# Group-normalised, quantised grouped convolution on one core: one transfer over all 128 partitions, and PSUM sets in rotation

## The chip, the cores and the metric

The kernel runs on one core of a Trainium2 chip. The metric is the time of one execution on the device in microseconds (us). The core has five engines that run side by side (TensorE "PE", VectorE "DVE", ScalarE "ACT", GpSimd "POOL", SyncE "SP"), and 16 DMA engines that move data between HBM and the on-chip memory SBUF. Transfers are issued here from two queues, SP's and ACT's. PSUM is the memory into which PE writes.

## The reference

The input `x` has shape (32, 512, 28, 28) in float32. It is group-normalised over 32 groups of 16 channels, and the result `v` goes through a grouped 1x1 convolution with 4 groups of 128 channels:

```python
v = group_norm(x, 32 groups, eps=1e-5)
xg = v.reshape(B, G, Cg, H, W)[:, [1, 2, 3, 0]]        # output group g reads input group g + 1
xa = round(clip((xg - lA) / (uA - lA), 0, 1) * 15) / 15
wq = (round(clip((w - lW) / (uW - lW), 0, 1) * 15) / 15 - 0.5) * 2
y  = einsum('bgihw,goi->bgohw', xa, wq)
out = x + relu(y * inv + (beta - mean * inv)) + v
```

51.4 MB are read and 51.4 MB are written. Everything passes through SBUF once.

## The kernel before

**Layout.** An image (one of the 32) has 512 channels of 784 values. Its four groups lie in `images[P, RING, G, HW]` with two channels of one group in one partition: a pair of neighbouring channels is 6272 contiguous bytes in HBM and in a partition. The 128 partitions are halved (LOW is 0 to 63, HIGH is 64 to 127), and the four slots of a partition are two pairs `y` of two channels `t`. LOW holds group 0 in pair 0 and group 3 in pair 1; HIGH holds group 1 in pair 0 and group 2 in pair 1 (`GROUPS`, L51). The distance in HBM from pair 0 to pair 1 differs between the halves, so each transfer covers one half: 64 partitions with two rows of 6272 bytes each (L234 loads, L214 stores). The first two images and the last one are moved in finer pieces (L222, L246).

**Ring.** 12 images (`RING`) fit in SBUF. `load(n)` (L229) waits from image 12 on until image n - 12 has been stored. Loads are issued by SP. Stores of images 0 to 29 are issued by ACT, and those of images 30 and 31 by SP after all the loads.

**Work for an image.** Mean and variance are taken on DVE (`bn_stats`, L517) and ACT (L274, L282), and are averaged over the channels of a norm group by small matmuls on PE for two images at a time (`average_means` L638, `average_deviations` L651). POOL turns them into coefficients. ACT and POOL quantise to integers (L310, L481), DVE caps them into `codes` (L532), PE multiplies (`multiply`, L679), and POOL (on the last three images ACT too) applies the affine part of the identity in place (L470, L318). At last DVE adds the rectified product onto the image (`finish`, L539), and the image is stored. The statistics run `AHEAD` = 5 images ahead of `finish`. On ACT the store of image n is issued after the statistics of image n + 5 or n + 6, which wait for that image's load.

**PE's order.** `multiply` is done twice for an image (t = 0 and 1), each 3 parts x 2 x 2 x 4 = 48 matmuls of 64 x 64 weights onto 392 columns, four of them on the four quarters of the array, and each half writes two of three PSUM sets. Which ones is said by `PSUM_SET` (L28): sets 0, 1, 2, 0 for the four outputs of an even image and 1, 2, 0, 1 for those of an odd one. An image after the first waits at t = 0 for `final` to reach 4n - (n mod 2) (L671): an even image for all four finishes of the image before, an odd one for three. At t = 1 each waits for the first finish of its own image. 28 of the 32 images are multiplied in a loop whose body holds two images and whose waits depend on a register `trip` (L707).

**Start.** Weights come in two transfers (L226), are quantised on DVE and sorted by four instructions of 128 x 128 (L578), and are turned by PE (L695).

Of the kernel before, what the change touches and what calls it, by code (L numbers as in the profile page):

```python
# [26 lines left out]

PSUM_SET = ((0, 1, 2, 0), (1, 2, 0, 1))  # L28

ORDER = (0, 2, 1, 3)  # L30
BODY = 2
SUBSETS = 4
# [3 lines left out]
def fused_norm_quantised_conv(nc, x, weight, limits, channel_params, out):  # L36
# [10 lines left out]


    HP = P // 2
    LOW, HIGH = slice(0, HP), slice(HP, P)  # L50
    GROUPS = ((LOW, slice(0, G, G - 1)), (HIGH, slice(1, G - 1)))  # L51

    def by_pairs(t):
        return t.rearrange("b (g i t) h w -> b g i (t h w)", g=G, t=2)

    x_v, out_v = by_pairs(x), by_pairs(out)
    w_v = weight.rearrange("(g i t) c -> g i (t c)", g=G, t=2)

# [39 lines left out]
    with ExitStack() as ctx:  # L98
# [106 lines left out]
        def wait_image(engine, n, g):  # L205
            if n < SINGLE:
                engine.wait_ge(first_loaded[n][g // 2], 2 * DMA)
            else:
                engine.wait_ge(x_loaded[n % RING], 2 * DMA * (n // RING + (1 if n % RING >= SINGLE else 0)))

        def store_image(engine, n):
            engine.wait_ge(final, G * n + G)
            for part, groups in GROUPS:
                engine.dma_start(out_v[n, groups].rearrange("y i f -> i y f"),  # L214
                                 pairs_of(images[part, n % RING])).then_inc(stored[n % RING], DMA)

        @block.sync
        def _(sync):
            for n in range(SINGLE):
                for y in range(2):  # L220
                    for part, groups in GROUPS:
                        sync.dma_start(pairs_of(images[part, n])[:, y],  # L222
                                       x_v[n, groups][y]).then_inc(first_loaded[n][y], DMA)
                if n == 0:
                    for part, groups in GROUPS:
                        sync.dma_start(pairs_of(w_raw[part]),  # L226
                                       w_v[groups].rearrange("y i f -> i y f")).then_inc(weights_in, DMA)

            def load(n):  # L229
                j = n % RING  # L230
                if n >= RING:
                    sync.wait_ge(stored[j], 2 * DMA * (n // RING))
                for part, groups in GROUPS:
                    sync.dma_start(pairs_of(images[part, j]),  # L234
                                   x_v[n, groups].rearrange("y i f -> i y f")).then_inc(x_loaded[j], DMA)

            for n in range(SINGLE, B):
                load(n)
            for n in range(ACT_STORES, B - 1):
                store_image(sync, n)  # L240
            j = (B - 1) % RING
            for k in range(G):
                y, t = ORDER[k] // 2, ORDER[k] % 2
                sync.wait_ge(final, G * (B - 1) + k + 1)
                for part, groups in GROUPS:
                    sync.dma_start(out_v[B - 1, groups][y][:, t * HW:(t + 1) * HW],  # L246
                                   images[part, j, ORDER[k]]).then_inc(stored[j], DMA)
            for j in range(RING):
                stores = len(range(j, B, RING)) + (G - 1 if j == (B - 1) % RING else 0)
                sync.wait_ge(stored[j], 2 * DMA * stores)  # L250

        @block.scalar
        def _(act):
# [5 lines left out]
            nc.scalar.activation(cols[:, 4], cols_ps[:, 8 * G:9 * G], ACT.Identity).then_inc(cols_done, 1)  # L259
            for part, groups in GROUPS:  # L260
                turned = cols_ps[part, 0:8 * G].rearrange("p (t k g) -> p k g t", t=2, k=4)
                nc.scalar.activation(cols[part, 0:4].rearrange("p k (y t) -> p k y t", t=2), turned[:, :, groups],
                                     ACT.Identity).then_inc(cols_done, 1)
# [238 lines left out]
        def _(dve):  # L502
# [31 lines left out]
            def finish(n, g):  # L534
                o = ORDER[g]
                if g % 2 == 0:
                    dve.wait_ge(multiplied, 2 * n + g // 2 + 1)
                two = images[:, n % RING, o].rearrange("p (h f) -> p h f", h=2)
                nc.vector.scalar_tensor_tensor(out=two, in0=prod[:, PSUM_SET[n % 2][g], :, 0:HALF], scalar=floor[:, o:o + 1],  # L539
                                               in1=two, op0=ALU.max, op1=ALU.add).then_inc(final, 1)  # L540
# [36 lines left out]
            for g in range(G):  # L577
                done = nc.vector.tensor_scalar(w_sorted[:, g % 2, :, 1 - g // 2], w_rest[:, g].rearrange("p (i s) -> p s i", s=2),  # L578
                                               bn[:, 3, g:g + 1], None, ALU.mult)
            done.then_inc(w_scaled, 1)  # L580
# [36 lines left out]
        def _(pe):  # L617
# [8 lines left out]


            def average_means(trip, v):
                k, u = stats_on_dve(v), trip + v
                pe.wait_ge(bn_summed, u + 1)  # L630
                pe.wait_ge(squared, squares_until(v) + trip * (squares_until(v + 1) - squares_until(v)))
                if v >= 1:
# [9 lines left out]
            def average_deviations(trip, v):  # L642
                u = trip + v
                pe.wait_ge(dev_done, u + 1)
                if v >= 1:
                    pe.wait_ge(std_done, u)
# [8 lines left out]

            def wait_affines(n, i, t):
                if i < B - HELPED:
                    pe.wait_ge(y_pool, G * n + 2 * t + 2)
                elif t == 0:
                    pe.wait_ge(y_pool, y_pool_until(i - 1) + 2)  # L660
                else:
                    pe.wait_ge(y_act, y_act_until(i))

            def multiply(trip, i, t):
                n, sets = BODY * trip + i, PSUM_SET[i % 2][2 * t:2 * t + 2]
                if t == 0:
                    pe.wait_ge(capped, n + 1)
                if i > 0 or t == 1:  # L670
                    pe.wait_ge(final, G * n + 1 if t == 1 else G * n - i % 2)  # L671
                for part in range(PARTS):
                    for s in range(2):
                        for h in range(2):
                            if (part, s, h) == (PARTS - 1, 1, 1):
                                wait_affines(n, i, t)
                            for y, inputs in ((0, HIGH), (1, LOW)):
                                for c, outputs in enumerate((LOW, HIGH)):
                                    done = nc.tensor.matmul(prod[outputs, sets[y], h, 0:HALF], w_t[inputs, part, t, s, outputs],  # L679
                                                            codes[inputs, i % 2, 2 * c + s, h * HALF:(h + 1) * HALF],  # L680
                                                            start=(part == 0 and s == 0), stop=(part == PARTS - 1 and s == 1))
                done.then_inc(multiplied, 1)

            def image_products(trip, i, more):
                if more and i % 2 == 0:
                    average_deviations(trip, (i + 2) // 2)
                multiply(trip, i, 0)
                if more and i % 2 == 1:
                    average_means(trip, (i + 3) // 2)
                multiply(trip, i, 1)  # L690

# [4 lines left out]
            turned.then_inc(w_turned, 1)  # L696
            average_means(0, 0)
            average_deviations(0, 0)
            pe.wait_ge(w_ready, 1)
            average_means(0, 1)  # L700
            multiply(0, 0, 0)
            average_deviations(0, 1)
            multiply(0, 0, 1)

            chained_images = B - 4
            assert chained_images % BODY == 0 and chained_images < B - HELPED
# [28 lines left out]
```

## Time and profile before

| | |
|---|---|
| median of 3 runs | 322.63 us (317.69 to 323.72) |
| the profiled execution | 316.4 us, of which its span is 314.7 us |
| busy share of the span | PE 65%, DVE 74%, ACT 68%, POOL 69% |
| DMA | 103.56 MB in the span, mean 329 GB/s |
| granted TensorE clock, mean | 0.907 |

The span is what the profiler saw from the first to the last instruction of the core; 1.7 us of the execution lie around it. The busy shares are averages over stages that differ: a stretch at the start in which little has arrived, a long stretch with a steady beat of two images, and an end in which only stores are left.

### The profile page before, as it was taken

The numbers are of one execution on the slowest core, as the hardware profiler recorded it, in microseconds if no ns is written. First come the engines' busy times: TensorE is split into PE (matmuls) and PEld (weight loads), VectorE is DVE, ScalarE is ACT, GpSimd is POOL, SyncE is SP. The second block draws the span as 40 slices with busy tenths as digits, with TensorE's granted clock in tenths as the row PEclk, the third lists the DMA queues.
The fourth block names the chain that finished last, engine by engine and source line by source line (L and its number), as shares of the span: only waits on it lengthen the run. The fifth ranks groups of instructions, "written<-read, shape, count | busy, mean of one in ns | idle before, by whom it ended". The sixth has DMA issues, their size and how long they took to land.

```text
span 314.7 us, 8243 instructions
## 1 busy us (share of the span) xinstructions
PE 203.8 (65%) x3336; PEld 141.0 (45%) x3336; DVE 232.7 (74%) x364; ACT 213.9 (68%) x394; POOL 217.8 (69%) x376
## 2 busy tenths in 40 slices
PE   1122397668586767877777777776858676875640
PEld 0022265455364545455545554554536354643430
DVE  1763567797988979697879897969798796957650
ACT  2222768878797878768797988796978859477000
POOL 5104287787979797959797989797887959696000
PEclk9999999797989989597979997979898698979995
DMA  7999999999999999999999999999999988899987
GB/s 173 231 222 216 215 216 217 270 344 362 398 398 398 398 397 402 401 399 401 395 404 408 411 412 414 408 419 408 409 404 406 404 258 196 187 254 237 244 201 228
DMA packets 19207, 103.56 MB, mean 329 GB/s; under 512 B 2258, under 2 KB 2530, under 8 KB 19170
## 3 DMA queue, kind: packets, MB, share of 16 engines
q1 hardware_dynamic: 10496, 54.86, 53.4%
q10 hardware_dynamic: 8674, 48.18, 44.1%
q8 instruction: 26, 0.43, 0.6%
q14 instruction: 11, 0.09, 0.1%
HBM read 51.65 MB, written 51.38 MB: 327 GB/s over the span
## 4 chain that ended last, share of the span: by engine, by line
PE 44%; DVE 26%; DMA 12%; issue 10%; SPq 3%; ACT 2%; POOL 0%; DVEq 0%; ACTq 0%; POOLq 0%
PE prod L679 39%; DVE images L539 17%; DMA images<-in_x 12%; DVE stats L517 8%; PE mean_ps L638 4%; SPq L222 2%; SPq L234 1%; ACT levels L310 1%; DVE sums L525 1%; ACT unused L274 1%; DVE codes L532 0%; SPq L226 0%; ACT unused L282 0%; DVEq L98 0%; PE var_ps L651 0%
## 5 line engine op out<-in xcount | busy, mean ns | idle before, releaser
L679 PE MATMUL prod<-codes,w_t 64*64 64x392 bf16 x3072 | 165.8, 370 | 51.5 <-DVE images L539 51.5
L539 DVE SCALAR_TENSOR_TENSOR images<-prod,floor,images 128x784 f32<-128x784 f32 x128 | 126.3, 1028 | 50.4 <-PE prod L679 50.3
L679 PEld LDWEIGHTS prod<-codes,w_t 64*64 64x64 bf16 x3072 | 105.0, 119 | 101.9 <-issue 39.2
L470 POOL TENSOR_SCALAR images<-images,coef 128x784 f32<-128x784 f32 x122 | 130.1, 1078 | 0.0
L310 ACT ACTIVATE levels<-images,coef 128x784 int16<-128x784 f32 x95 | 91.4, 1028 | 2.2 <-POOL coef L461 2.2
L517 DVE BATCH_NORM_STATS2 stats<-images 128x6 f32<-128x392 f32 x136 | 66.9, 553 | 17.7 <-DMA images<-in_x 17.7
L274 ACT ACTIVATE unused<-images 128x784 bf16<-128x784 f32 x60 | 50.9, 849 | 40.3 <-DMA images<-in_x 35.8
L282 ACT ACTIVATE unused<-images,sums 128x784 bf16<-128x784 f32 x60 | 56.1, 938 | 0.1
L427 POOL TENSOR_TENSOR dev<-stats,gmean 128x16 f32<-128x16 f32 x16 | 3.7, 229 | 50.6 <-ACT gmean L290 50.6
L532 DVE TENSOR_SCALAR codes<-levels 128x3136 bf16<-128x3136 int16 x32 | 34.1, 1064 | 1.4 <-ACT levels L310 1.4
L481 POOL TENSOR_SCALAR levels<-images,coef 128x784 int16<-128x784 f32 x33 | 33.6, 1020 | 0.1
L638 PE MATMUL mean_ps<-sums,avg 128*128 128x2 f32 x68 | 11.3, 273 | 27.4 <-DVE sums L525 22.2
L638 PEld LDWEIGHTS mean_ps<-sums,avg 128*128 128x128 f32 x68 | 10.0, 214 | 33.2 <-DVE sums L525 22.6
L290 ACT ACTIVATE gmean<-mean_ps 128x4 f32<-128x4 f32 x16 | 2.7, 169 | 25.1 <-PE mean_ps L638 25.1
L651 PE MATMUL var_ps<-sums,avg_n 128*128 128x4 f32 x64 | 12.9, 271 | 7.8 <-POOL dev_sum L435 7.8
L651 PEld LDWEIGHTS var_ps<-sums,avg_n 128*128 128x128 f32 x64 | 10.6, 207 | 13.9 <-POOL dev_sum L435 13.3
L433 POOL TENSOR_TENSOR dev<-dev 128x32 f32<-128x32 f32 x16 | 12.1, 757 | 1.3
L652 PE MATMUL var_ps<-dev_sum,avg 128*128 128x4 f32 x64 | 12.7, 268 | 0.0
L282 ACT ACTIVATION_READ_ACCUMULATOR unused<-images,sums 128x1 f32 x60 | 11.4, 190 | 0.0
L274 ACT ACTIVATION_READ_ACCUMULATOR unused<-images 128x1 f32 x60 | 11.2, 187 | 0.0
L652 PEld LDWEIGHTS var_ps<-dev_sum,avg 128*128 128x128 f32 x64 | 10.9, 214 | 0.0
L638 PE MATMUL mean_ps<-sums,avg_one 128*128 128x2 f32 x60 | 9.3, 258 | 0.0
(71 smaller groups left out, 83.2 us busy)
## 6 DMA issues: line engine op xcount, KB each, us to landing
images<-in_x SPq DMA_DIRECT2D x60, 784.0 KB, 30.2
out<-images ACTq DMA_DIRECT2D x60, 784.0 KB, 12.5
images<-in_x SPq DMA_DIRECT2D x8, 392.0 KB, 8.1
out<-images SPq DMA_DIRECT2D x2, 784.0 KB, 7.4
out<-images SPq DMA_DIRECT2D x8, 196.0 KB, 3.5
w_raw<-in_weight SPq DMA_DIRECT2D x2, 128.0 KB, 7.4
rows<-in_channel_params ACTq DMA_DIRECT2D x1, 8.0 KB, 1.6
limit_row<-in_limits ACTq DMA_DIRECT2D x1, 0.0 KB
```

Source lines behind the costliest of these rows:

```text
L274: nc.scalar.activation(unused[:, g % 2], images[:, n % RING, g], ACT.Identity, scale=1.0 / HW, accum_out=sums[:, 0, j, g:g + 1]).then_inc( ...
L282: nc.scalar.activation(unused[:, g % 2], images[:, n % RING, g], ACT.Square, scale=-1.0, bias=sums[:, 0, j, g:g + 1], accum_out=sums[:, 1, ...
L310: nc.scalar.activation(levels[:, n % 2, g], images[:, n % RING, g], ACT.Relu, bias=coef[:, u % 2, 1, 0, G * j + g:G * j + g + 1], scale=co ...
L470: nc.gpsimd.tensor_scalar(here, here, coef[:, u % 2, 0, 1, G * j + o:G * j + o + 1], coef[:, u % 2, 1, 1, G * j + o:G * j + o + 1], ALU.mu ...
L481: nc.gpsimd.tensor_scalar(levels[:, n % 2, g], images[:, n % RING, g], coef[:, u % 2, 0, 0, G * j + g:G * j + g + 1], coef[:, u % 2, 1, 0, ...
L517: nc.vector.bn_stats(two, images[:, n % RING, g, h * HALF:(h + 1) * HALF]).then_inc(bn_done, 1)
L532: nc.vector.tensor_scalar(codes[:, n % 2], levels[:, n % 2], 0.0, TOP, ALU.max, ALU.min).then_inc(capped, 1)
L539: nc.vector.scalar_tensor_tensor(out=two, in0=prod[:, PSUM_SET[n % 2][g], :, 0:HALF], scalar=floor[:, o:o + 1], in1=two, op0=ALU.max, op1= ...
L638: done = nc.tensor.matmul(mean[:, :, y], avg[:] if q < k else avg_one[:], sums[:, 0, :, q], start=(t == 0), stop=(t == 1))
L651: nc.tensor.matmul(var, avg_n[:], squares[:, :, :, t], start=(t == 0), stop=False)
L652: done = nc.tensor.matmul(var, avg[:], spread[:, :, :, t], start=False, stop=(t == 1))
L679: done = nc.tensor.matmul(prod[outputs, sets[y], h, 0:HALF], w_t[inputs, part, t, s, outputs], codes[inputs, i % 2, 2 * c + s, h * HALF:(h ...
```

## The change

Groups are renumbered by halves: LOW holds groups 0 and 1 in pairs 0 and 1, HIGH holds groups 2 and 3. Pair `y` of both halves is now one regular pattern in HBM (`r`, two values that lie 256 channels apart, then 64 rows of 6272 bytes), and it is moved by one transfer with one row on each of 128 partitions, where before a transfer had two rows on each of 64. The number and the size of the transfers for an image stay: two of 784 KB in and two out. The last image is stored in four transfers, not eight.

The PSUM set of the output g of image n is (4n + g) mod 3. `multiply` waits for `final` to reach 4n + 2t - 1, for all images alike. PE's loop is written out. The weights are sorted by eight instructions on 64 partitions in place of four on 128, and the order in which the four quarters of the PE array are used changes.

```diff
-PSUM_SET = ((0, 1, 2, 0), (1, 2, 0, 1))
-    GROUPS = ((LOW, slice(0, G, G - 1)), (HIGH, slice(1, G - 1)))
+    HALVES = (LOW, HIGH)
     def by_pairs(t):
-        return t.rearrange("b (g i t) h w -> b g i (t h w)", g=G, t=2)
+        return t.rearrange("b (r y i t) h w -> b y r i (t h w)", r=2, y=2, t=2)
-    w_v = weight.rearrange("(g i t) c -> g i (t c)", g=G, t=2)
+    w_v = weight.rearrange("(r y i t) c -> y r i (t c)", r=2, y=2, t=2)
         def wait_image(engine, n, g):
             if n < SINGLE:
-                engine.wait_ge(first_loaded[n][g // 2], 2 * DMA)
+                engine.wait_ge(first_loaded[n][g // 2], DMA)
         def store_image(engine, n):
-            for part, groups in GROUPS:
-                engine.dma_start(out_v[n, groups].rearrange("y i f -> i y f"),
-                                 pairs_of(images[part, n % RING])).then_inc(stored[n % RING], DMA)
+            for y in range(2):
+                engine.dma_start(out_v[n, y], pairs_of(images[:, n % RING])[:, y]).then_inc(stored[n % RING], DMA)
...
-                    for part, groups in GROUPS:
-                        sync.dma_start(pairs_of(images[part, n])[:, y],
-                                       x_v[n, groups][y]).then_inc(first_loaded[n][y], DMA)
+                    sync.dma_start(pairs_of(images[:, n])[:, y], x_v[n, y]).then_inc(first_loaded[n][y], DMA)
...
-                for part, groups in GROUPS:
-                    sync.dma_start(pairs_of(images[part, j]),
-                                   x_v[n, groups].rearrange("y i f -> i y f")).then_inc(x_loaded[j], DMA)
+                for y in range(2):
+                    sync.dma_start(pairs_of(images[:, j])[:, y], x_v[n, y]).then_inc(x_loaded[j], DMA)
...
-                for part, groups in GROUPS:
-                    sync.dma_start(out_v[B - 1, groups][y][:, t * HW:(t + 1) * HW],
-                                   images[part, j, ORDER[k]]).then_inc(stored[j], DMA)
+                sync.dma_start(out_v[B - 1, y][:, :, t * HW:(t + 1) * HW],
+                               images[:, j, ORDER[k]]).then_inc(stored[j], DMA)
...
-                done = nc.vector.tensor_scalar(w_sorted[:, g % 2, :, 1 - g // 2], w_rest[:, g].rearrange("p (i s) -> p s i", s=2),
-                                               bn[:, 3, g:g + 1], None, ALU.mult)
+                y, t = g // 2, g % 2
+                for part, inputs in ((LOW, y), (HIGH, 1 - y)):
+                    done = nc.vector.tensor_scalar(w_sorted[part, t, :, inputs],
+                                                   w_rest[part, g].rearrange("p (i s) -> p s i", s=2),
+                                                   bn[part, 3, g:g + 1], None, ALU.mult)
...
-                n, sets = BODY * trip + i, PSUM_SET[i % 2][2 * t:2 * t + 2]
-                if i > 0 or t == 1:
-                    pe.wait_ge(final, G * n + 1 if t == 1 else G * n - i % 2)
+                first = G * n + 2 * t
+                if first >= SETS - 1:
+                    pe.wait_ge(final, first + 2 - SETS)
-                            for y, inputs in ((0, HIGH), (1, LOW)):
-                                for c, outputs in enumerate((LOW, HIGH)):
-                                    done = nc.tensor.matmul(prod[outputs, sets[y], h, 0:HALF], w_t[inputs, part, t, s, outputs],
-                                                            codes[inputs, i % 2, 2 * c + s, h * HALF:(h + 1) * HALF],
+                            for y in range(2):
+                                for r, outputs in enumerate(HALVES):
+                                    inputs = HALVES[(r + y) % 2]
+                                    done = nc.tensor.matmul(prod[outputs, (first + y) % SETS, h, 0:HALF],
+                                                            w_t[inputs, part, t, s, outputs],
+                                                            codes[inputs, n % 2, 2 * (1 - y) + s, h * HALF:(h + 1) * HALF],
...
-            for trip in range(chained_images // BODY):
-                for i in range(1, 1 + BODY):
-                    image_products(trip, i, True)
-            for n in range(1 + chained_images, B):
-                image_products(0, n, False)
+            for n in range(B):
+                u = n // 2 + 1
+                if n % 2 == 0 and n and u < PAIRS:
+                    average_deviations(u)
+                multiply(n, 0)
+                if n == 0:
+                    average_deviations(1)
+                if n % 2 == 1 and u + 1 < PAIRS:
+                    average_means(u + 1)
+                multiply(n, 1)
```

## Rows read from the trace of the kernel before

**Rows 1.** The page: busy tenths and DMA in 40 slices of 7.9 us.

```profile
PEclk9999999797989989597979997979898698979995
DMA  7999999999999999999999999999999988899987
GB/s 173 231 222 216 215 216 217 270 344 362 398 398 398 398 397 402 401 399 401 395 404 408 411 412 414 408 419 408 409 404 406 404 258 196 187 254 237 244 201 228
```

**Rows 2.** Busy time by stretch: busy us (count) per engine, clock, DMA share, GB/s.

```profile
12.00:48.00 36.00, 16.20 (x132) 11.84 (x132) 19.88 (x43) 15.60 (x33) 13.17 (x34) 1.00 1.02 219
160.00:200.00 40.00, 28.97 (x521) 19.92 (x517) 34.05 (x51) 34.09 (x65) 35.51 (x58) 0.91 1.02 410
306.00:315.00 9.00, 0.00 (x0) 0.00 (x0) 0.00 (x0) 0.00 (x0) 0.00 (x0) 0.56 0.71 214
```

**Rows 3.** The chain that ended last, its first wait for a load.

```profile
11.80 36.62 DMA images<-in_x
```

**Rows 4.** Timeline of DVE: statistics that wait for loads, and the last finish.

```profile
25.88 1.97 DVE L517 BATCH_NORM_STATS2 stats<-images 128x6 f32<-128x392 f32 x4 [3.56 <-DMA images<-in_x]
33.31 2.91 DVE L517 BATCH_NORM_STATS2 stats<-images 128x6 f32<-128x392 f32 x6 [4.45 <-DMA images<-in_x]
...
303.92 1.98 DVE L539 SCALAR_TENSOR_TENSOR images<-prod,floor,images 128x784 f32<-128x784 f32 x2 [1.35 <-PE prod L679]
```

**Rows 5.** The page: DMA issues, count, KB each, median us from issue to landing.

```profile
images<-in_x SPq DMA_DIRECT2D x60, 784.0 KB, 30.2
out<-images ACTq DMA_DIRECT2D x60, 784.0 KB, 12.5
images<-in_x SPq DMA_DIRECT2D x8, 392.0 KB, 8.1
out<-images SPq DMA_DIRECT2D x2, 784.0 KB, 7.4
out<-images SPq DMA_DIRECT2D x8, 196.0 KB, 3.5
```

**Rows 6.** Timeline of SP's queue: start, us and count of issued transfers.

```profile
0.79 2.49 SPq L222 DMA_DIRECT2D images<-in_x  x4
3.32 1.30 SPq L226 DMA_DIRECT2D w_raw<-in_weight  x2
...
31.49 9.65 SPq L234 DMA_DIRECT2D images<-in_x  x1
```

**Rows 7.** Timeline around the start of an even image (PE, DVE).

```profile
151.26 2.19 PE L679 MATMUL prod<-codes,w_t 64*64 64x392 bf16 x48 [1.23 <-DVE images L539]
...
157.50 1.98 DVE L539 SCALAR_TENSOR_TENSOR images<-prod,floor,images 128x784 f32<-128x784 f32 x2 [0.51 <-PE prod L679]
...
158.41 0.36 PE L652 MATMUL var_ps<-dev_sum,avg 128*128 128x4 f32 x2
...
159.62 3.49 PE L679 MATMUL prod<-codes,w_t 64*64 64x392 bf16 x48 [0.85 <-DVE images L539]
...
167.66 2.19 PE L679 MATMUL prod<-codes,w_t 64*64 64x392 bf16 x48 [1.23 <-DVE images L539]
```

**Rows 8.** The page: costliest groups, busy us and mean ns of one.

```profile
L679 PE MATMUL prod<-codes,w_t 64*64 64x392 bf16 x3072 | 165.8, 370 | 51.5 <-DVE images L539 51.5
```

**Rows 9.** Instructions of line 578: shortest, median and longest ns.

```profile
L578 DVE TENSOR_SCALAR w_raw<-w_rest,bn x4: 281/282/287, 13.4 to 14.0; 128x128 f32<-128x128 f32 x4
```

**Rows 10.** The page: instruction queues of the DMA engines; packets, MB, share.

```profile
q8 instruction: 26, 0.43, 0.6%
q14 instruction: 11, 0.09, 0.1%
```

**Rows 11.** Who waited for whom: us in total, times, longest.

```profile
DVE stats L517 <- DMA images<-in_x: 17.7, 7, 4.5
PEld prod L679 <- issue: 39.2, 30, 2.5
```

More of the change, by code:

```diff
@@ L220, in _ @@
                 for y in range(2):
-                    for part, groups in GROUPS:
-                        sync.dma_start(pairs_of(images[part, n])[:, y],
-                                       x_v[n, groups][y]).then_inc(first_loaded[n][y], DMA)
+                    sync.dma_start(pairs_of(images[:, n])[:, y], x_v[n, y]).then_inc(first_loaded[n][y], DMA)
                 if n == 0:
-                    for part, groups in GROUPS:
-                        sync.dma_start(pairs_of(w_raw[part]),
-                                       w_v[groups].rearrange("y i f -> i y f")).then_inc(weights_in, DMA)
+                    for y in range(2):
+                        sync.dma_start(pairs_of(w_raw[:])[:, y], w_v[y]).then_inc(weights_in, DMA)
             def load(n):
@@ L244, in _ @@
                 sync.wait_ge(final, G * (B - 1) + k + 1)
-                for part, groups in GROUPS:
-                    sync.dma_start(out_v[B - 1, groups][y][:, t * HW:(t + 1) * HW],
-                                   images[part, j, ORDER[k]]).then_inc(stored[j], DMA)
+                sync.dma_start(out_v[B - 1, y][:, :, t * HW:(t + 1) * HW],
+                               images[:, j, ORDER[k]]).then_inc(stored[j], DMA)
             for j in range(RING):
-                stores = len(range(j, B, RING)) + (G - 1 if j == (B - 1) % RING else 0)
-                sync.wait_ge(stored[j], 2 * DMA * stores)
+                stores = 2 * len(range(j, B, RING)) + (G - 2 if j == (B - 1) % RING else 0)
+                sync.wait_ge(stored[j], DMA * stores)
         @block.scalar
@@ L259, in _ @@
             nc.scalar.activation(cols[:, 4], cols_ps[:, 8 * G:9 * G], ACT.Identity).then_inc(cols_done, 1)
-            for part, groups in GROUPS:
+            for r, part in enumerate(HALVES):
                 turned = cols_ps[part, 0:8 * G].rearrange("p (t k g) -> p k g t", t=2, k=4)
-                nc.scalar.activation(cols[part, 0:4].rearrange("p k (y t) -> p k y t", t=2), turned[:, :, groups],
+                nc.scalar.activation(cols[part, 0:4].rearrange("p k (y t) -> p k y t", t=2), turned[:, :, 2 * r:2 * r + 2],
                                      ACT.Identity).then_inc(cols_done, 1)
@@ L538, in finish @@
                 two = images[:, n % RING, o].rearrange("p (h f) -> p h f", h=2)
-                nc.vector.scalar_tensor_tensor(out=two, in0=prod[:, PSUM_SET[n % 2][g], :, 0:HALF], scalar=floor[:, o:o + 1],
+                nc.vector.scalar_tensor_tensor(out=two, in0=prod[:, (G * n + g) % SETS, :, 0:HALF], scalar=floor[:, o:o + 1],
                                                in1=two, op0=ALU.max, op1=ALU.add).then_inc(final, 1)
@@ L625, in _, with average_means @@
                              stop=True).then_inc(cols_turned, 1)
-            def average_means(trip, v):
-                k, u = stats_on_dve(v), trip + v
+            def average_means(u):
+                k = stats_on_dve(u)
                 pe.wait_ge(bn_summed, u + 1)
-                pe.wait_ge(squared, squares_until(v) + trip * (squares_until(v + 1) - squares_until(v)))
-                if v >= 1:
+                pe.wait_ge(squared, squares_until(u))
+                if u >= 1:
                     pe.wait_ge(gmean_done, u)
@@ L640, in average_means, with average_deviations @@
                 done.then_inc(mean_done, 1)
-            def average_deviations(trip, v):
-                u = trip + v
+            def average_deviations(u):
                 pe.wait_ge(dev_done, u + 1)
-                if v >= 1:
+                if u >= 1:
                     pe.wait_ge(std_done, u)
@@ L653, in average_deviations, with wait_affines, multiply @@
                 done.then_inc(var_done, 1)
[L656 to L666, printed above, removed]
-                n, sets = BODY * trip + i, PSUM_SET[i % 2][2 * t:2 * t + 2]
+            def wait_affines(n, t):
+                pe.wait_ge(y_pool, y_pool_until(n - 1) + min(2 * t + 2, G - affine_on_act(n)))
+                if t == 1 and affine_on_act(n):
+                    pe.wait_ge(y_act, y_act_until(n))
+            def multiply(n, t):
+                first = G * n + 2 * t
                 if t == 0:
                     pe.wait_ge(capped, n + 1)
-                if i > 0 or t == 1:
-                    pe.wait_ge(final, G * n + 1 if t == 1 else G * n - i % 2)
+                if first >= SETS - 1:
+                    pe.wait_ge(final, first + 2 - SETS)
                 for part in range(PARTS):
@@ L675, in multiply @@
                             if (part, s, h) == (PARTS - 1, 1, 1):
-                                wait_affines(n, i, t)
-                            for y, inputs in ((0, HIGH), (1, LOW)):
-                                for c, outputs in enumerate((LOW, HIGH)):
-                                    done = nc.tensor.matmul(prod[outputs, sets[y], h, 0:HALF], w_t[inputs, part, t, s, outputs],
-                                                            codes[inputs, i % 2, 2 * c + s, h * HALF:(h + 1) * HALF],
+                                wait_affines(n, t)
+                            for y in range(2):
+                                for r, outputs in enumerate(HALVES):
[3 more added lines that the diff above has]
+                                                            codes[inputs, n % 2, 2 * (1 - y) + s, h * HALF:(h + 1) * HALF],
                                                             start=(part == 0 and s == 0), stop=(part == PARTS - 1 and s == 1))
                 done.then_inc(multiplied, 1)
[L684 to L690, printed above, removed]
             pe.wait_ge(w_scaled, 1)
@@ L696, in _ @@
             turned.then_inc(w_turned, 1)
-            average_means(0, 0)
-            average_deviations(0, 0)
+            average_means(0)
+            average_deviations(0)
             pe.wait_ge(w_ready, 1)
[L700 to L706, printed above, removed]
-            for trip in range(chained_images // BODY):
-                for i in range(1, 1 + BODY):
-                    image_products(trip, i, True)
-            for n in range(1 + chained_images, B):
-                image_products(0, n, False)
+            average_means(1)
+            for n in range(B):
[8 more added lines that the diff above has]
+                multiply(n, 1)
 _LIMITS = ["L0_conv_lW", "L0_conv_uW", "L0_conv_lA", "L0_conv_uA"]
```

1 line of the change is left out of this document (removed).

## The prediction, made before the kernel was run

> **What bounds the kernel now.** I read the page's 40 slices first. They show three stages of the DMA engines. Up to about 56 us, where only loads run, they move some 216 GB/s with every engine busy. From 63 to 250 us they move 395 to 419 GB/s, again all busy, and from 252 us on 187 to 258 GB/s [rows 1]. The table by stretch says the same with a second digit: 219 GB/s at a DMA share of 1.02, then 410 GB/s at 1.02 [rows 2]. So one engine moves 219 / 16 = 13.7 GB/s while loads are alone and 410 / 16 = 25.6 GB/s (best slice 419 / 16 = 26.2) while loads and stores run together. In the middle PE has 29.0 of 40 us, DVE 34.1, ACT 34.1 and POOL 35.5: no compute engine is full, and the beat is held by PE and DVE waiting for each other, two images in 167.66 - 151.26 = 16.40 us [rows 7], close to what the DMA engines could do at best: 4 x 1.606 MB / 410 GB/s = 15.7 us. The chain that ended last starts with 36.6 us of waiting for loads [rows 3], and the statistics on DVE wait 17.7 us for them in all [rows 11], in pieces as in [rows 4]. The last finish ends at 303.92 + 1.98 = 305.9 us and the span at 314.7, so 8.8 us of stores follow. DMA therefore decides at both ends and is almost full between them; whatever takes rate from it shows in the time at once.
>
> **The change, part by part.**
>
> *Transfers.* Bytes stay: 60 x 784 KB + 8 x 392 KB in and 62 x 784 KB + 8 x 196 KB out [rows 5] are 2 x 51.38 MB, with 0.26 MB of weights 103.0 MB. What changes is the shape. Before, both sides of each data transfer have 64 as their first (outermost) count: 64 partitions in SBUF, 64 pairs of channels in HBM. After, SBUF's side begins with 128 partitions, and HBM's with r, which takes two values, because 256 channels lie between the halves and the 128 rows don't form one regular run; `i` with its 64 comes second. A transfer is spread over engines before any byte moves, by cutting it along an index; I take it that this is the outermost one and that both sides must be cut alike. Before that gives 64, enough for all 16 engines, and the DMA share of 1.02 fits it [rows 2]. After, it gives two shares, one for each r, and two engines would do everything that 16 do now. No row shows a transfer with so small a first count, so its price has two bounds: 16 engines (below, a rival), and two. I take two, since the code has nothing on HBM's side ahead of the 2 that could be cut finer.
>
> The Trainium skill ("DMA: Bandwidth & Descriptors", sections "Why a DMA increments its semaphore by 16 and not by 1" and "Rules for kernel authors") has this as a rule: the number of engines is the largest one up to 16 that divides the slowest dimension, other than 1, of both access patterns, and an outermost dimension below 16 confines the whole transfer. By it k is 2 here. The trace agrees only as far as it goes (64, and all engines busy); no run here shows a small k.
>
> *What two engines cost.* At 26.2 GB/s each, 103.0 MB take 103.0 / 52.4 = 1966 us; at 25.6 GB/s each 103.0 / 51.2 = 2012 us. One image takes 1.606 / 52.4 = 31 us in and as much out, against about 7 us of work on ACT (68% of 314.7 us over 32 images, by the table of shares) and a beat of 8.2 us before. Loads run ahead by up to 12 images, the statistics by 5, so all compute lies beneath transfers. At the start loads run alone for 6 images, until the first store; at the end stores of the images that are still in the ring follow one another. To the sum come about 1 us before the first issue [rows 6], 2 us for the last landing and the 1.7 us around the span: 1966 + 5 = 1971 to 2012 + 5 = 2017. With no crowd of 16 the upper rate is nearer; I take 1990.
>
> *Queues.* The counts stay, so SP and ACT issue as many as before (0.62 us each when nothing blocks, [rows 6]: 2.49 us for four), except for the last image, four fewer. A single load issue held SP for 9.65 us where its queue was full [rows 6]. With 64 rows per engine in one transfer in place of 8, this will be the rule: 64 x 6272 B / 26.2 GB/s = 15.3 us for one transfer. Behind a blocked SP are only loads. Behind a store that is blocked on ACT wait the quantisation and the sums of the next images, with copies of means for POOL and PE. That is one or two issues of up to 15 us for an image, doubled where loads share the engines, against 62 us of transfers: covered, as long as a transfer is queued while ACT works. If the cover is gone, at most ACT's 7 us an image, 32 x 7 = 224 us, are added.
>
> *PSUM sets.* An even image's t = 0 starts after both of DVE's finishes (157.50 + 1.98 = 159.48, PE starts at 159.62) though the last small matmul ends at 158.41 + 0.36 = 158.77 [rows 7]. It would start after the first finish: 0.85 us earlier, 15 times, 12.8 us; odd images and t = 1 keep their waits. With DMA as the bound it is worth 0.
>
> *PE's loop and tiles.* 48 matmuls take 2.19 us at full clock [rows 7], 46 ns each, though one takes 370 ns [rows 8]: four overlap or more. The new order still uses all four quarters in turn. If they stopped overlapping, 96 x 370 ns = 35.5 us an image, still under 62; if they overlap better, nothing. Written out, the program is longer: the instruction queues moved 0.52 MB [rows 10]; ten times that would be 5.2 MB, 5% of the traffic, spread over the run; at the least nothing. A stall of PE's issue before a block (39.2 us in 30 times, [rows 11]) may go or grow. All under the transfers: 0.
>
> *Weights.* Four more DVE instructions of 0.28 us [rows 9], at most 1.1 us, once, in a start in which DVE waits 17.7 us for loads: 0. The waits for one transfer where there were two change nothing by themselves.
>
> **The rivals.**
>
> *A. Two engines, but slower while one direction is alone (chance 0.19).* The 13.7 GB/s of an engine in the load stretch could belong to the engine (a queue that runs alone) and not to the shape. Then 6 images at the start and 6 to 12 at the end pass at 27.4 GB/s: 12 x 1.606 = 19.3 MB cost 704 in place of 368 us, 18 images 504 us more: 2326 to 2494, centre 2380. For it: both unshared stretches are slow, 219 and 214 GB/s [rows 2]. Against: in both, each transfer touches one half of the partitions, which would explain the same rate, and the new transfers touch both.
>
> *B. All 16 engines go on (chance 0.16); this ends on the other side.* If the cut is made by partitions, or along any index, the load stretch loses its limit of 219 GB/s, since each transfer reaches all partitions. The start then gains at most the 17.7 us that DVE waits there [rows 11], say 15. Half of the 8.8 us of stores at the end is 4. The middle gains 12.8 us by the PSUM sets, cut to 15 x (16.4 - 15.7) = 10 by the DMA engines. Sum 29: 316.4 - 29 = 287 us. It decides from 13 engines on: 12 give 103.0 / (12 x 0.0262) = 328 us. The profile speaks for it with the halved rate at both ends, which the shape of 64 partitions would explain. Against it: nothing shows how 128 rows in two runs are cut.
>
> The Trainium skill ("SBUF — State Buffer", section "Door 1: The DMA port swizzle") says that partitions 0 to 63 reach 8 of 16 ports, about 218 GB/s, and 128 partitions all 16; the trace's 219 GB/s agrees. By that rule alone the change is faster, as in B.
>
> *C. Only one direction is confined (chance 0.03).* If only the source's first count matters, or only the destination's, loads alone or stores alone run on two engines: 51.4 / 52.4 = 981 us, with start and end about 1000 us. Nothing in the profile speaks for a difference between the sides.
>
> **How the numbers follow.** Two engines at the full rate 0.62, A 0.19, B 0.16, C 0.03. The predicted time is that of the first, 1990 us. My trust in the two engines comes from the code's shape and from the evenness of the existing split; it isn't more than 0.81 because no row has the case. The range begins at 1940, a little below the sum at the best slice (an engine may go up to 26.6 GB/s undisturbed: 103.0 / 53.2 = 1936), and ends at 2500, the end of A, which also holds a good part of the 224 us that an uncovered ACT would add. It leaves out B and C, 0.19. The likeliest case's own range is 1940 to 2100. In the comparison with before a difference of 2% (6 us) can about be told from none, given runs from 317.69 to 323.72. Slower by more: the first, A, C and none of B, 0.84. Of B 0.14 is faster by more and 0.02 within it.
>
> **What would show it.** DMA share: if two of 16 engines work, the mean share is 2 / 16 = 0.12 in every slice, and GB/s about 52 throughout; under A 27 at both ends; under B a share near 1 and about 400 GB/s from the first slices. A 784 KB transfer lands no sooner than 15.3 us after its issue, and loads from SP's full queue much later than 30.2 us. The first loads, which took 8.1 us to land [rows 5], land 15 us apart; each image takes 62 us. In the list of waits, ACT and DVE wait for loads most, and the waits of PE for L539 are gone for even images. ACT's queue shows store issues of 10 us and more. PE is idle for most of the time; what clock it is granted then is hidden too. The prediction is wrong if the share is near 1, or if GB/s in the middle is far from 52: above it, the engines are more than two; below it, an engine alone is slower than 25.6.

## The result and the profile after

The changed kernel takes 1947.64 us (1947.51 to 1947.84 in 4 runs) against 322.17 us before (317.69 to 323.72): 6.09 times as long, with an interval of 6.04 to 6.14. The profiled execution took 1947.76 us with a span of 1946.0.

The page of the kernel after: busy times, the slices as in [rows 1] (one is now 48.7 us), and an instruction queue as in [rows 10]:

```profile
PE 280.0 (14%) x3336; PEld 175.7 (9%) x3336; DVE 233.4 (12%) x368; ACT 213.6 (11%) x394; POOL 210.6 (11%) x376
...
PEclk9998555555555555555555555555555555556555
DMA  1111111111111111111111111111111111111111
GB/s 49 53 54 53 53 53 54 53 54 54 54 53 53 54 53 54 53 54 54 54 54 53 53 54 53 54 54 53 54 53 53 54 53 54 54 53 53 53 53 48
...
q8 instruction: 26, 0.43, 0.1%
```

The same bytes now pass at 53 to 54 GB/s in every slice but the first (49) and the last (48), where [rows 1] had 216 and then 400. The compute engines are busy for as long as before, apart from PE: 280 us for 204. From the fifth slice on it stood idle for long between its blocks and was granted about half its full clock (0.54 in the stretch below), mostly the lower level of 1.2 GHz, at which 48 matmuls take up to 4.14 us in place of 2.19 [rows 7]. The table by stretch (columns as in [rows 2]: length, PE, PEld, DVE, ACT, POOL, clock, DMA share, GB/s) gives the share's second digit:

```profile
400.00:800.00 400.00, 65.66 (x736) 40.25 (x736) 45.67 (x68) 46.62 (x84) 44.33 (x75) 0.54 0.13 54
...
1850.00:1940.00 90.00, 0.00 (x0) 0.00 (x0) 0.00 (x0) 0.00 (x0) 0.00 (x0) 0.50 0.13 52
```

0.13 of 16 engines is 2. The share alone could also be 16 engines at an eighth of their time; the next experiment speaks for two that are always busy. The second row lies behind the last finish, which ends at 1831.44 + 1.98 = 1833.4 us, where only stores are left: one direction alone goes as fast as both. Of the waits (who waited for what: us in total, times, longest) the longest are now:

```profile
DVE stats L509 <- DMA images<-in_x: 1293.4, 34, 48.0
ACT unused L266 <- DMA images<-in_x: 823.4, 20, 49.1
...
PE prod L669 <- DVE images L531: 764.8, 37, 55.3
```

DVE waited 17.7 us for loads before [rows 11]. The timeline around one image, DVE, ACT and ACT's queue:

```profile
1000.28 1.97 DVE L509 BATCH_NORM_STATS2 stats<-images 128x6 f32<-128x392 f32 x4 [43.48 <-DMA images<-in_x]
...
1007.57 29.30 ACTq L212 DMA_DIRECT2D out<-images  x1
...
1036.90 31.82 ACTq L212 DMA_DIRECT2D out<-images  x1
...
1060.54 1.97 DVE L509 BATCH_NORM_STATS2 stats<-images 128x6 f32<-128x392 f32 x4 [47.43 <-DMA images<-in_x]
...
1068.84 0.86 ACT L266 ACTIVATE unused<-images 128x784 bf16<-128x784 f32 x1 [55.77 <-issue]
```

From one image's statistics on DVE to the next it is 60.3 us. The two store issues hold ACT's queue for 29.30 and 31.82 us, until 1036.90 + 31.82 = 1068.7 us; ACT's share of the next image's statistics starts only then, 8.3 us after DVE's. In all, ACT stood 653.7 us before such statistics in waits that the profile puts down to "issue", besides the 823.4 us for loads.

### The profile page after: what moved, and what is told of

The parts are those of the page before. It is cut to its first block and busy times, and to the rows that moved or that the text cites. A ratio compares the mean times of both kernels' runs of the same rounds, so it can differ in the third digit from the quotient of the medians.

```text
span 1946.0 us, 8242 instructions
## 1 busy us (share of the span) xinstructions
PE 280.0 (14%) x3336; PEld 175.7 (9%) x3336; DVE 233.4 (12%) x368; ACT 213.6 (11%) x394; POOL 210.6 (11%) x376
## 5 line engine op out<-in xcount | busy, mean ns | idle before, releaser
L669 PE MATMUL prod<-codes,w_t 64*64 64x392 bf16 x3072 | 224.7, 465 | 784.6 <-DVE images L531 764.8
L266 ACT ACTIVATE unused<-images 128x784 bf16<-128x784 f32 x60 | 50.9, 849 | 1477.1 <-DMA images<-in_x 823.4
L669 PEld LDWEIGHTS prod<-codes,w_t 64*64 64x64 bf16 x3072 | 121.1, 149 | 874.0 <-DVE images L531 729.7
L462 POOL TENSOR_SCALAR images<-images,coef 128x784 f32<-128x784 f32 x122 | 120.3, 999 | 26.5 <-ACT levels L302 26.5
L632 PE MATMUL mean_ps<-sums,avg 128*128 128x2 f32 x68 | 16.6, 351 | 679.8 <-issue 596.5
L444 POOL TENSOR_TENSOR newt<-rough 128x4 f32<-128x4 f32 x16 | 3.9, 241 | 753.2 <-DVE rough L541 753.2
L632 PEld LDWEIGHTS mean_ps<-sums,avg 128*128 128x128 f32 x68 | 15.7, 323 | 685.4 <-issue 658.0
L453 POOL TENSOR_TENSOR coef<-scaled,coef_add 128x32 f32<-128x32 f32 x16 | 15.4, 965 | 1.3
L645 PEld LDWEIGHTS var_ps<-dev_sum,avg 128*128 128x128 f32 x64 | 15.3, 293 | 0.0
L632 PE MATMUL mean_ps<-sums,avg_one 128*128 128x2 f32 x60 | 15.0, 352 | 0.0
L632 PEld LDWEIGHTS mean_ps<-sums,avg_one 128*128 128x128 f32 x60 | 14.7, 333 | 0.0
```

The source lines that it names most:

```text
L266: nc.scalar.activation(unused[:, g % 2], images[:, n % RING, g], ACT.Identity, scale=1.0 / HW, accum_out=sums[:, 0, j, g:g + 1]).then_inc( ...
L462: nc.gpsimd.tensor_scalar(here, here, coef[:, u % 2, 0, 1, G * j + o:G * j + o + 1], coef[:, u % 2, 1, 1, G * j + o:G * j + o + 1], ALU.mu ...
L645: done = nc.tensor.matmul(var, avg[:], spread[:, :, :, t], start=False, stop=(t == 1))
L669: done = nc.tensor.matmul(prod[outputs, (first + y) % SETS, h, 0:HALF], w_t[inputs, part, t, s, outputs], codes[inputs, n % 2, 2 * (1 - y) ...
```

## The experiments

### The first count on HBM's side, changed alone

```diff
-        return t.rearrange("b (r y i t) h w -> b y r i (t h w)", r=2, y=2, t=2)
+        return t.rearrange("b (r y i t) h w -> b y r i (t h w)", r=4, y=2, t=2)
```

and the same with r = 8 and r = 16. Partitions, rows, bytes and the number of transfers stay those of the kernel after. Channels come to other partitions than the weights assume, so these kernels do the same work but compute another function. The two small transfers of the weights keep their first count of 2 in all of them.

> As r16 with r = 4 (again another output). One engine for each value of r: 1947.6 us at 2 engines is 103.0 MB at 52.9 GB/s, so 4 engines give 103.0 / 105.8 = 974 us, and a DMA share of 0.25. If the split is all or nothing (a count under 16 always gives two engines, or one for each half), it stays at 1950 us.

> As r16 with r = 8 (another output): 8 engines. By the count alone 103.0 MB at 8 x 26.6 = 213 GB/s give 484 us, plus some for the start and end, about 495. Theory 1 of rows128 (engines meet at the SBUF side) makes the load stage slow even with 8 engines, well below 200 GB/s, and the total longer. Theory 2 (a limit of 220 to 236 GB/s shared by all) leaves 8 engines just under the limit: about 210 GB/s in every slice.

> The kernel after with r = 16 in the view of the input and the output: HBM's side of each transfer begins with 16 values that lie 32 channels apart, then 8 rows; partitions, row size, number of transfers and bytes are those of the kernel after. Channels then come to other partitions than the weights assume, so the output is another function; the work is the same. If the first count sets the number of engines, all 16 work and the time is rival B's, 287 us (275 to 305), with about 400 GB/s from the first slices. If the new shape (128 partitions with one row) is slow for another reason, it stays near 1950 us.

| first count | time, us | GB/s in the middle | DMA share there |
|---|---|---|---|
| 2 (the kernel after) | 1947.6 | 53 to 54 | 0.13 |
| 4 | 985.6 (one execution) | 107 | 0.26 |
| 8 | 522.9 (one execution) | 212 | 0.51 |
| 16 | 298.9 (296.2 to 300.4) | 416 | 1.02 |

The table's last two columns for r = 4, 8 and 16 (r = 4 from 400 to 800 us, the others from 160 to 200 us):

```profile
400.00:800.00 400.00, 108.12 (x1344) 68.45 (x1344) 90.45 (x136) 83.45 (x160) 87.01 (x145) 0.59 0.26 107
...
160.00:200.00 40.00, 22.45 (x292) 14.28 (x296) 20.40 (x31) 16.79 (x35) 19.92 (x34) 0.70 0.51 212
...
160.00:200.00 40.00, 28.95 (x568) 20.19 (x568) 36.68 (x57) 33.98 (x64) 34.00 (x53) 1.00 1.02 416
```

The rate doubles with the count and so does the share, up to 16. So the first count of HBM's side sets how much of the 16 engines works, and with r = 16 alone nothing is left of the slowdown: nothing else in the change makes the kernel slow. That it is this count of engines that works, each all the time, is the plain reading (share and rate for one engine, 26 to 27 GB/s, fit at every step); the profile doesn't name the engines. r = 4 came within 12 us of the expected 974; r = 8 missed the expected 495 by 28 us (more on it below).

The dependence is also the rule of the Trainium skill ("DMA: Bandwidth & Descriptors", "Why a DMA increments its semaphore by 16 and not by 1"): the largest k up to 16 that divides both slowest dimensions. With 128 on SBUF's side and 2, 4, 8, 16 on HBM's the runs agree with it.

r = 16 takes 298.9 us, 0.934 of before (0.925 to 0.943), not the 287 of rival B. Its load stage tells why; the table by stretch, 12 to 48 us, of r16:

```profile
12.00:48.00 36.00, 9.33 (x64) 7.64 (x68) 17.89 (x43) 12.24 (x24) 7.76 (x23) 1.00 1.02 232
```

232 GB/s at a full share (the first store is issued at 60 us), hardly more than the 219 of [rows 2], though each transfer touches all 128 partitions. So "each transfer reaches all partitions" was not enough to lift that limit.

### The transfers cut by halves again, the rest of the change kept

```diff
...
-            for y in range(2):
-                engine.dma_start(out_v[n, y], pairs_of(images[:, n % RING])[:, y]).then_inc(stored[n % RING], DMA)
+            for r, part in enumerate(HALVES):
+                engine.dma_start(out_v[n, :, r].rearrange("y i f -> i y f"),
+                                 pairs_of(images[part, n % RING])).then_inc(stored[n % RING], DMA)
...
```

and so for the loads and the weights.

> The kernel after with its transfers cut by partition halves again (64 partitions with two rows each), all else of the change kept: new places of the groups, PSUM sets in rotation, PE's loop written out, eight weight instructions. If the first count of 2 on HBM's side is the whole cause, the time comes back to that of before, 322 us, or to as little as 305 us if the rotation gives its 12.8 us. The rival, that the rest of the change costs something too, gives more than 325 us.

308.22 us (305.75 to 310.92), 0.963 of before (0.956 to 0.970). The slowdown is gone whole, and the rest of the change is a gain. Its part that could be one is the rotation, so that was taken back in the next run:

```diff
...
-                if first >= SETS - 1:
-                    pe.wait_ge(final, first + 2 - SETS)
+                if n > 0 or t == 1:
+                    pe.wait_ge(final, G * n + 1 if t == 1 else G * n - n % 2)
...
```

with `PSUM_SET` again choosing the sets in `multiply` and `finish`.

> The run halves (308.2 us) with PSUM_SET and the waits of before put back; places of groups, PE's order of quarters and the written-out loop stay as after. If the rotation of the sets is what makes halves faster than before, this is back at 320 us. If the written-out loop or the order of the quarters did it, it stays at 308 us.

319.45 us (316.59 to 324.69), 0.998 of before (0.992 to 1.004). The rotation is worth 319.45 - 308.22 = 11.2 us; the written-out loop and the new order of the quarters are worth nothing that can be measured. PE's timeline in `halves` shows where it comes from:

```profile
155.61 0.36 PE L650 MATMUL var_ps<-dev_sum,avg 128*128 128x4 f32 x2
155.91 2.19 PE L674 MATMUL prod<-codes,w_t 64*64 64x392 bf16 x48
```

The even image's matmuls follow directly on the last small one (155.91, where that ends at 155.97); in [rows 7], and again with the old sets (160.18 us in `halves_oldsets`), PE stood for 0.85 us waiting for DVE's second finish. Over the whole run PE waited 41.5 us for DVE before these matmuls in `halves` and 53.9 us in `halves_oldsets`, 12.4 us less. The mean granted clock of TensorE was higher too, 0.930 against 0.901 in the two profiled executions, and how much of the 11.2 us is the one and how much the other no run separates. With these waits shorter, DMA holds the chain that ended last for 74% of the span, against PE's 44% and DVE's 27% with the old sets.

### Only the loads confined

```diff
...
-    x_v, out_v = by_pairs(x), by_pairs(out)
+    x_v, out_v = by_pairs(x), by_pairs(out, 16)
```

with r as an argument of `by_pairs`, 2 when not given.

> The kernel after with r = 16 for the output only; the input keeps r = 2 (another output). If the first count matters on the side that is read, as it does on either side, loads alone are on two engines, 51.6 MB at 52.9 GB/s: 976 us and a few us of tail. If only the side that is written counts (rival C in one form), loads go at full rate and the time is near 290 us.

1123.6 us (one execution): a miss by 148. The direction of the transfer doesn't matter: HBM's side is the source of a load and the destination of a store, and it set the count for loads alone here and for both in the kernel after, so rival C falls. What the 976 left out is that stores spread over 16 engines also lie on the two that carry the loads: (51.6 / 2 + 51.4 / 16) MB = 29.0 MB on each of them, at 26.7 GB/s (107 / 4 at r = 4) 1087 us, with the last image's compute and stores behind it. The page's rates change between two levels:

```profile
GB/s 48 52 53 53 54 53 53 104 53 154 53 150 56 54 154 53 154 53 55 152 54 154 54 91 115 53 154 54 130 77 54 154 53 154 53 54 154 53 184 234
```

53 to 54 is two engines' loads alone; the other slices hold stores besides. Which engines carried what isn't in the profile, so the sum is an argument that fits, not one that a row shows.

### A regular run of 128 rows

```diff
-        return t.rearrange("b (r y i t) h w -> b y r i (t h w)", r=2, y=2, t=2)
+        return t.rearrange("b (y p t) h w -> b y p (t h w)", y=2, t=2)
...
```

> The kernel after, but each transfer takes 256 neighbouring channels, so that HBM's side is one regular run of 128 rows (another output: channels sit on other partitions than the weights assume). r16, with 16 values of 8 rows each, kept 232 to 236 GB/s while loads ran alone, against 219 before, where rival B wanted 400. Theory 1: r16 gives each engine 8 neighbouring partitions, and engines get in each other's way at the SBUF side; a regular run of 128 is dealt out otherwise and reaches 400 GB/s in the load stage, with a total of about 285 us. Theory 2: loads alone are held at 220 to 236 GB/s by something that all engines share, whatever the shape; then the stage and the time stay as in r16, 299 us.

276.44 us (276.19 to 276.85), 0.862 of before (0.857 to 0.868). The stretch from 12 to 48 us and the page's rates of rows128:

```profile
12.00:48.00 36.00, 18.60 (x181) 13.50 (x182) 26.19 (x57) 20.88 (x42) 17.71 (x38) 1.00 1.02 417
...
GB/s 237 295 418 423 423 418 422 406 240 316 422 372 424 419 422 422 418 424 420 421 422 421 421 423 422 421 425 415 422 422 423 422 409 220 288 405 225 241 242 240
```

Loads alone (the first store is issued at 49 us) reach 417 GB/s, against 232 for r16 with the same partitions, row size, count of transfers and engines. Theory 2, a limit shared by whatever loads there are, falls. What differs from r16 is the view of HBM: one unbroken run of 128 rows in place of 16 runs of 8 with gaps between them, and with it, perhaps, which rows fall to which engine. These two runs don't separate the two. With loads early enough, POOL holds the chain that ended last for 63% of the span, where in r16 DMA held 73% of it.

The Trainium skill ("SBUF — State Buffer", "Door 1: The DMA port swizzle") gives about 218 GB/s for 64 partitions and 436 for 128, as what long transfers approach. 219 before agrees, 417 here lies 4% under it, and r16's 232 on 128 partitions doesn't follow from the number of partitions alone. r8 doesn't fit the simple form of theory 1 either, since its load stage is slow only at first. Stretches of r8 (clock, share, GB/s at the end), all before its first store at 69 us:

```profile
12.00:16.00 4.00, 0.00 (x0) 0.00 (x0) 1.49 (x3) 1.79 (x3) 0.00 (x0) 1.00 0.25 74
...
20.00:24.00 4.00, 0.00 (x0) 0.00 (x0) 2.59 (x7) 0.00 (x0) 0.00 (x0) 1.00 0.50 149
...
32.00:36.00 4.00, 1.44 (x7) 1.47 (x8) 3.47 (x8) 1.99 (x4) 0.00 (x0) 1.00 0.50 210
```

Over the first 26 us it has 127 GB/s. Part of that is a drop of the share to 0.25, which comes after the weights were issued; their two transfers may be on two engines, which would leave the others idle, but no row shows it. The rest is not a slow start of transfers as such: at a share of 0.5 the loads pass 145 to 172 GB/s up to 28 us and 201 to 213 behind that, while the two engines of the kernel after have 52 to 53 GB/s from 4 us on. Since the same view of HBM later gives 210, the gaps in it alone don't hold these eight engines down. Eight engines that met at the SBUF side and then fell out of step would look so. But r16 has 232 and 236 GB/s in the stretches 12 to 48 and 48 to 60 us and doesn't recover, and it stays open how r16 and r8 deal out their rows. The slow first 26 us are worth at most 26 x (1 - 127 / 213) = 10 of the 28 us by which r8 missed.

### Two queues in the load stage

```diff
...
+            for n in range(SINGLE):
+                for y in range(2):
+                    act.dma_start(pairs_of(images[HIGH, n])[:, y], x_v[n, y, 1]).then_inc(first_loaded[n][y], DMA)
+            for n in range(SINGLE, 4):
+                act.dma_start(pairs_of(images[HIGH, n]),
+                              x_v[n, :, 1].rearrange("y i f -> i y f")).then_inc(x_loaded[n], DMA)
...
```

SP keeps the loads of the LOW half of these images.

> The run halves (308.2 us) with the loads of the HIGH half of images 0 to 3 issued on ACT's queue at its start, beside those of the LOW half on SP's. If the load stage is slow because one queue at a time fills one half of the partitions, the two streams together pass 219 GB/s by far in the first 20 us, image 3 is there at about 20 us in place of 33, and the time falls by up to 10 us. If all loads share one limit, image 3 comes at about 33 us as before, and the time stays within 3 us of 308.

One execution took 300.99 us, and since a single one can lie some us off, the same kernel was run several times more:

> The kernel two_queues once more with rounds. One execution took 301.0 us. It was faster than halves (308.2 us) by 7 us, and its first slices moved up to 289 GB/s while loads ran alone. If that is the effect of the two streams, it is at 298 to 303 us again; if it was the spread of single executions, it is at 306 to 310 us.

304.04 us (302.21 to 305.89), between the two ranges that were expected, so part of the 7 us was the spread of single executions. The medians lie 4 us below `halves`, but the two ratios to before, 0.953 (0.946 to 0.960) and 0.963 (0.956 to 0.970), overlap in their intervals, so the gain in time is small and barely shown. The rate does rise: the best slice of the load stage had 289 GB/s in the first run and 304 in the second. DVE takes up image 3 at 29.62 and 28.89 us, without waiting for it, where in `halves` it waited until 33.14; the forecast of about 20 us doesn't come out. Two streams into the two halves help, far less than one regular run.

### A version that keeps the reference

```diff
...
+    PIECES = (((slice(0, P), slice(0, P)),), ((LOW, slice(3 * HP, 4 * HP)), (HIGH, slice(2 * HP, 3 * HP))))
...
-        return t.rearrange("b (r y i t) h w -> b y r i (t h w)", r=2, y=2, t=2)
+        return t.rearrange("b (q t) h w -> b q (t h w)", t=2)
...
-                engine.dma_start(out_v[n, y], pairs_of(images[:, n % RING])[:, y]).then_inc(stored[n % RING], DMA)
+                for part, rows_ in PIECES[y]:
+                    engine.dma_start(out_v[n, rows_], pairs_of(images[part, n % RING])[:, y]).then_inc(stored[n % RING], DMA)
...
-                                    inputs = HALVES[(r + y) % 2]
+                                    inputs = HALVES[1 - y]
...
```

> A version that computes the reference: the groups sit where they sat before (LOW 0 and 3, HIGH 1 and 2), pair 0 of both halves is then one regular run of 128 rows (groups 0 and 1) and moves in one transfer, as in rows128; pair 1 moves in two transfers of 64 rows. Rotation of the PSUM sets and the written-out loop are kept. rows128 took 276 us and halves 308. If the rate in the stages with one direction depends on each transfer's own partitions, the load stage passes half its bytes at 420 and half at 219 GB/s, 288 GB/s on average, and the total lies in the middle, 288 to 297 us. If one slow transfer in the queue holds up the regular ones behind it, it is 305 us or more.

294.27 us (292.70 to 299.92), 0.923 of before (0.917 to 0.929): faster than both kernels. The stretch from 12 to 48 us of mixed:

```profile
12.00:48.00 36.00, 18.20 (x216) 13.70 (x220) 25.06 (x52) 21.32 (x42) 17.67 (x39) 1.00 1.02 263
```

263 GB/s, somewhat under the 288 of the average. Half the bytes in regular runs bring 308.2 - 294.3 = 14 of the 32 us that all of them bring in rows128. All of them can't be had in this layout: the two regular runs of an image hold groups 0 and 1, and 2 and 3, so that every output group sits in the other half than its input, and only two of the four quarters of the PE array would be used.

## Why the prediction was right, step by step

**Two engines.** Right: the share is 0.13, the rate 53 to 54 GB/s, and r = 4, 8, 16 show that the first count of HBM's side sets it.

**Their rate.** 1990 was forecast, 1947.6 came, 2.1% less; the lower sum of 1971 was 1.2% too long. The mis-sized term is the rate of an engine: 26.2 GB/s was the best slice with 16 engines at work, while the full slices here have 53 to 54, up to 27 for each. I had put 26.6 as the most for the range's lower end, which no row showed, and the choice of the middle between 26.2 and 25.6 for the forecast was on the wrong side: 16 engines together have 416 / 16 = 26.0 each, and a few have more, 107 / 4 = 26.8 at r = 4 and 212 / 8 = 26.5 at r = 8. One image in and out took 60.3 us for 62, and the first two loads, which DVE waits for, are there 34.08 - 18.89 = 15.2 us apart, for 15.

**Compute and queues hidden.** Right. ACT's issues took 29.3 and 31.8 us, twice the 15.3, as the text had it for engines that loads share. In the image shown ACT came 8.3 us late to the next one by them, and still the transfers covered it: DMA's share never fell, so the 224 us of an uncovered ACT didn't appear. The page's table of issues has no landing time for the large transfers, so the forecast on loads from a full queue can't be read.

**PSUM sets, loop, quarters, weights.** Their price in the changed kernel was 0, as forecast. The 12.8 us, or 10 under the limit of DMA, that the rotation would be worth without that cover measured 11.2. The instruction queue moved 0.43 MB after as before [rows 10]: the bound of ten times as much for the written-out loop had no ground. The sign given for the sets held where they act and was too wide as worded. PE's timeline in the changed kernel, an even image at t = 0 and then at t = 1:

```profile
1014.43 4.13 PE L669 MATMUL prod<-codes,w_t 64*64 64x392 bf16 x48
...
1072.12 4.14 PE L669 MATMUL prod<-codes,w_t 64*64 64x392 bf16 x48 [53.56 <-DVE images L531]
```

At t = 0 it no longer waits for DVE. At t = 1 it waits for the first finish of its own image, a wait that the rotation keeps, and this one grew from about 1 us to over 50 us, since DVE reaches that finish only behind statistics that wait for a load (1060.54 us above) and behind ACT, held by its store issue (1068.84 us). Such waits make up most of the 764.8 us. They are hidden like the rest.

**Rival A** was wrong. The last stretch has 52 GB/s with stores alone, and the slices at the start, with loads alone, 49 and then 53. The halved rate of [rows 2] isn't an engine's limit in one direction. (The centre of its range was also off: between 2326 and 2494 it is 2410, not 2380.)

**Rival B** is what the change would have been with 16 engines, and the forecast of 287 us lies between its two forms, 298.9 (r16) and 276.4 (rows128). The error of its step was to take the rate of the load stage from the number of partitions. With all 128 in both, it depends on the shape of HBM's side, by more than 22 us of total time.

**Rival C** fell with load2_store16.

## What to carry to other kernels

Before a transfer is widened to more partitions, write down the counts of both sides, slowest first: the share of the engines at work here followed the first count on HBM's side when that was 2, 4, 8 or 16, and a leading 2 cost a factor of 6. The DMA share shows it at once: here 0.13, with loads waited for everywhere, meant few engines, not few bytes. A good idea hidden beneath such a cost is found by undoing one part alone: the rotation of three PSUM sets brought 3.5%, and moving half the bytes in regular runs of 128 rows another 4%.

## What the runs showed that had not been expected

Two transfers' shapes with the same share of engines, partitions, rows and bytes differ nearly by two when one direction runs alone: 232 GB/s for 16 runs of 8 rows and 417 GB/s for one run of 128. Together with the other direction both reach 416 and 421, so a profile of the middle of a kernel doesn't show it. Why the two differ is not shown. The mean granted clock of TensorE was 0.995 in rows128 and 0.907 before, with the same matmuls in less time; what raised it wasn't studied.
